# Two-layer cross-attention kernel: in the first layer, GpSimd issues the regrouping transfers, both halves of a projection share a step, and a batch's closing operations run some steps later

## The reference, cut to what matters

```
# layer 0, for each of 8 batches: x, kv are (256 channels, 512 positions), 16 heads of 16 channels
q = Wq @ x + bq;  k = Wk @ kv + bk;  v = Wv @ kv + bv
attn = softmax(q^T k / sqrt(16))                  # 512 x 512 for each head
mean = attn @ v;  ex2 = attn @ (v * v)
std  = sqrt(relu(ex2 - mean * mean))
x    = normalise(x) * std + mean                  # masked normalisation of x over positions
# layer 1, for each batch, x is (256 positions, 512 features), 16 heads of 32
x = x + self_attention(layernorm(x));  x = x + cross_attention(layernorm(x), ctx)
x = x + gelu(layernorm(x) @ w1 + b1) @ w2 + b2
```

## Time and profile before

| what | us |
|---|---|
| runs (3), median | 1876.81 |
| runs, lowest and highest | 1871.81, 1877.14 |
| profiled execution, its own time | 1867.23 |
| profiled execution, span of the trace | 1865.4 |
| last `maxima` of the first layer starts at | 727.8 |
| TensorE, VectorE, ScalarE, GpSimd busy | 1669.1, 1276.1, 1064.0, 342.7 |

### The profile page before, as it was taken

One profiled execution on the slowest core, in us unless ns is written; L12 is line 12 of the kernel. 1 busy time (PEld: TensorE's weight loads), 2 busy tenths in 40 slices (PEclk: granted clock), 3 DMA queues, 4 the chain that ended last, 5 costly groups with the idle time before them and its releaser, 6 DMA issues.

```text
span 1865.4 us, 30868 instructions
## 1 busy us (share of the span) xinstructions
PE 1669.1 (89%) x10589; PEld 1126.5 (60%) x10589; DVE 1276.1 (68%) x2758; ACT 1064.0 (57%) x2351; POOL 342.7 (18%) x435
## 2 busy tenths in 40 slices
PE   4888888887788889799999989999999899999999
PEld 2433333333333333478887877878888788888888
DVE  1666676676757766588899989999999864232322
ACT  1455556555555546678787787887878752121111
POOL 0001111112111113232223222223332130000000
PEclk7998898999989899999999999999999899999999
DMA  5343343444343433233223253333333240000000
GB/s 173 114 129 110 125 117 116 120 125 125 120 138 112 128 93 102 73 96 75 69 69 91 70 136 95 100 86 100 97 93 82 82 136 23 1 23 1 23 4 31
DMA packets 108955, 167.97 MB, mean 90 GB/s; under 512 B 23680, under 2 KB 39424, under 8 KB 108672
## 3 DMA queue, kind: packets, MB, share of 16 engines
q1 hardware_dynamic: 96784, 140.74, 26.4%
q0 software_dynamic: 9472, 20.99, 4.4%
q10 hardware_dynamic: 2544, 4.26, 0.8%
HBM read 72.06 MB, written 34.60 MB: 57 GB/s over the span
## 4 chain that ended last, share of the span: by engine, by line
PE 44%; DVE 20%; SPq 13%; DMA 10%; issue 7%; ACT 5%; POOL 1%; ACTq 0%; DVEq 0%; POOLq 0%
PE ps L1931 9%; PE ps L1905 7%; PE ps L526 6%; DMA ring<-rows 5%; DVE at_t L1383 4%; PE ps L1254 4%; DVE at_t L1388 4%; SPq L298 4%; SPq L366 3%; PE ps L1264 3%; PE ps L503 3%; SPq L332 2%; DMA rows<-shares_of 2%; PE ps L1203 2%; PE ps L1910 2%
## 5 line engine op out<-in xcount | busy, mean ns | idle before, releaser
L600 DVE TENSOR_REDUCE nmax<-ps 128x2 f32<-128x1024 f32 x256 | 311.2, 1221 | 204.5 <-PE ps L503 202.5
L772 ACT ACTIVATE prob<-ps 128x1024 f32<-128x1024 f32 x256 | 261.8, 1023 | 271.0 <-PE ps L512 267.5
L1591 ACT ACTIVATE at_prob<-at_t,at_nmax 128x256 f32<-128x256 f32 x512 | 256.6, 505 | 85.4 <-DVE at_nmax L1388 74.1
L526 PE MATMUL ps<-prob,v 128*64 128x512 f32 x1024 | 299.3, 665 | 0.9
L503 PE MATMUL ps<-ring 64*128 64x512 f32 x512 | 137.3, 533 | 117.7 <-issue 55.5
L1388 DVE CUSTOM_DVE_ANT_0 at_t<-at_t,at_off 128x256 f32<-128x256 f32 x512 | 232.3, 490 | 8.8
L503 PEld LDWEIGHTS ps<-ring 64*128 64x128 f32 x512 | 51.3, 196 | 275.2 <-issue 196.2
L2090 DVE CAST mlp_h_hi<-mlp_h 128x512 fp32r<-128x512 f32 x64 | 28.4, 444 | 212.0 <-ACT mlp_h L2002 180.0
L1749 POOL TENSOR_TENSOR at_low<-at_low,at_high 128x512 fp32r<-128x512 f32 x64 | 87.1, 1361 | 468.1 <-DVE at_high L1417 468.1
L2002 ACT ACTIVATE mlp_h<-ps,b 128x512 f32<-128x512 f32 x48 | 33.1, 690 | 218.4 <-PE ps L1905 218.4
L1203 PE MATMUL ps<-ident,at_prob 128*128 128x128 f32 x1024 | 156.9, 276 | 0.0
(11 more groups left out here) (215 smaller groups left out, 3747.1 us busy)
## 6 DMA issues: line engine op xcount, KB each, us to landing
ring<-rows SPq DMA_DIRECT2D x62, 512.0 KB, 4.7
rows<-shares_of SPq DMA_DIRECT2D x90, 256.0 KB
at_k_stack<-at_high SPq DMA_DIRECT2D x256, 64.0 KB, 2.5
at_q_stack<-at_high POOLq DMA_DIRECT2D x128, 64.0 KB, 2.5
at_q_stack<-at_high SPq DMA_DIRECT2D x128, 64.0 KB, 2.7
at_q_stack<-at_low SPq DMA_DIRECT2D x128, 64.0 KB, 2.1
at_k_stack<-at_low POOLq DMA_DIRECT2D x128, 64.0 KB, 2.4
c_in<-in_ctx SPq DMA_DIRECT2D x8, 512.0 KB, 4.6
```

What stands on the lines that cost most here:

```text
L526: mm = eng.matmul(ps[2 * QD * k:2 * QD * (k + 1), VB, :], v[:, c, HG * G + 2 * p + k, :], prob[:, M % PROBS, k, :], start=(c == 0), stop=( ...
L600: eng.tensor_reduce(nmax[:, n % 2, j, 2 * p:2 * p + 2], ps[:, at:at + 2, :], AX, ALU.max, negate=True).then_inc(s_max, 1)
L772: eng.activation(prob[:, M % PROBS, :, :], ps[:, ST:ST + 2, :], ACT.Exp, scale=float(HD0) ** -0.5).then_inc(s_exp, 1)
L1591: ins = eng.activation(prob[:, m % 2, i, :], t[:, p, i, :], ACT.Exp, scale=-1.0, bias=nmax[:, m % 4, i:i + 1], accum_out=z[:, T % 2, j, 2 ...
```

## The change

It touches only the first layer. Five things:

1. The two halves of a q projection both go into step 3, those of a k projection into step 6.
2. `regroup` becomes a function of the engine. GpSimd issues it for groups 0 to 29 (n < 60), SyncE for the last two groups, with semaphores of their own.
3. In the list of SyncE both `rows_out` stand at the end of the even group; `rows_in("q")` of the next group but one opens the odd group, ahead of `tops_in`; the other three `rows_in` follow directly. `shares_in` moves ahead of `tops_in`, and `far_out` ahead of `shares_out`.
4. The closing operations of a batch move to later steps on VectorE and ScalarE.
5. GpSimd's list interleaves regroups with its tensor operations.

```diff
-        if s in (2, 3, 5, 6) and w % 2 == 0 and w // 2 + 1 < PAIRS:
-            return [("q" if s < 4 else "k", w // 2 + 1, ((s + 1) % 3,))]
+        if s in (3, 6) and w % 2 == 0 and w // 2 + 1 < PAIRS:
+            return [("q" if s == 3 else "k", w // 2 + 1, (0, 1))]
...
+    def regroup(eng, n):
+        b, G, p = n // (2 * NG), n // 2 % NG, n % 2
+        eng.wait_ge(s_vout, n + 1)
...
+        done = (s_re if n < 2 * (GROUPS - 2) else s_last_re)[n % OUTS]
...
         for w in range(GROUPS + 3):
-            n, b, ahead = w - 2, w // NG - 1, w // 2 + 1
+            b, ahead = w // NG - 1, w // 2 + 1
+            if w % NG == 2 and b >= 0:
+                shares_in(b)
+            if w % 2 and ahead < PAIRS:
+                rows_in("q", 2 * ahead)
             if 0 <= w - 1 < GROUPS:
                 tops_in(w - 1)
-            if w % NG == 2 and b >= 0:
-                shares_in(b)
-            if 0 <= n < GROUPS:
-                regroup(2 * n)
+            if GROUPS <= w < GROUPS + 2:
+                regroup(eng, 2 * (w - 2))
             lead(w, False)
+            if GROUPS <= w < GROUPS + 2:
+                regroup(eng, 2 * (w - 2) + 1)
+            if w % 2 and ahead < PAIRS:
+                rows_in("k", 2 * ahead)
+                rows_in("q", 2 * ahead + 1)
+                rows_in("k", 2 * ahead + 1)
+            if w % NG == 2 and b + 2 < NB:
+                far_out(b + 2)
             if w % NG == 2 and b >= 0:
                 shares_out(b)
-            if w % NG == 2 and b + 2 < NB:
-                far_out(b + 2)
-            if w % 2 and ahead < PAIRS:
+            if w % 2 == 0 and ahead < PAIRS:
+                rows_out("q", ahead)
                 rows_out("k", ahead)
-                rows_in("q", 2 * ahead)
-                rows_in("k", 2 * ahead)
...
-            if 0 <= n < GROUPS:
-                regroup(2 * n + 1)
-            if w % 2 and ahead < PAIRS:
-                rows_in("q", 2 * ahead + 1)
-                rows_in("k", 2 * ahead + 1)
-            if w % 2 == 0 and ahead < PAIRS:
-                rows_out("q", ahead)
...
# VectorE
-                if w % NG == 2 and 0 <= b - 1 < NB and s == 3:
+                if w % NG == 2 and 0 <= b - 1 < NB and s == 5:
                     shares(b - 1)
-                if w % NG == 3 and 0 <= b - 1 < LAST - 1 and s == 5:
-                    positive_variance(b - 1)
-                if w % NG == 0 and 0 <= b - 2 < LAST - 1 and s == 2:
+                if w % NG == 0 and 0 <= b - 2 < LAST and s == 0:
+                    positive_variance(b - 2)
+                if w % NG == 0 and 0 <= b - 2 < LAST and s == (5 if w < GROUPS else 3):
                     normal_x(b - 2)
-                if w % NG == 1 and 0 <= b - 2 < LAST - 1 and s in (4, 5):
-                    last_mask(b - 2, s - 4)
...
+                if w % NG == 1 and 0 <= b - 2 < LAST and s in ((5, 6) if w < GROUPS else (2, 3)):
+                    last_mask(b - 2, (s + 1) % 3)
# ScalarE
-                if s == 3 and w % NG == 3 and 0 <= b - 1 < LAST - 1:
+                if s == 4 and w % NG == 3 and 0 <= b - 1 < LAST:
                     mean_squared(b - 1)
-                if s == 6 and w % NG == 3 and 0 <= b - 1 < LAST - 1:
-                    roots(b - 1)
...
+                if s == (2 if w < GROUPS else 1) and w % NG == 0 and 0 <= b - 2 < LAST:
+                    roots(b - 2)
# GpSimd
+        squares(0)
         for w in range(GROUPS):
+            n, b = w - 2, w // NG
+            if w % NG == 3 and 0 <= b - 1 < LAST:
                 finish_shares(b - 1, 0)
                 finish_shares(b - 1, 1)
+            if n >= 0:
+                regroup(eng, 2 * n)
+            if w % NG == 3 and 0 <= b - 1 < LAST:
                 finish_variance(b - 1)
             if w % NG == 0 and 0 < b < NB:
                 squares(2 * b)
+            if w % NG == 2 and b < NB:
+                squares(2 * b + 1)
+            if n >= 0:
+                regroup(eng, 2 * n + 1)
+            if w % NG == 0 and 0 <= b - 2:
                 finish_x(b - 2, 0)
                 finish_x(b - 2, 1)
```

More of the change, by code:

```diff
@@ L203, in layer0 @@
         s_re = [sem(f"re{k}") for k in range(OUTS)]
+        s_last_re = [sem(f"last_re{k}") for k in range(OUTS)]
         s_mask = sem("mask")
@@ L256, in regrouped, with all_regrouped @@
         def regrouped(n, k):
-            return (n - k + OUTS) // OUTS * 6 * DMA
+            times, by_pool = (n - k + OUTS) // OUTS, 2 * (GROUPS - 2) // OUTS
+            return [(s_re[k], min(times, by_pool) * 6 * DMA)] \
+                + ([(s_last_re[k], (times - by_pool) * 6 * DMA)] if times > by_pool else [])
+        def all_regrouped(eng, n):
+            for k in range(OUTS):
+                for done, value in regrouped(n, k):
+                    eng.wait_ge(done, value)
         def rows_of(i):
@@ L274, in layer0 @@
             "values out": [(s_vout, 2 * GROUPS)],
-            "regroups": [(s_re[k], regrouped(2 * GROUPS - 1, k)) for k in range(OUTS)],
+            "regroups": [x for k in range(OUTS) for x in regrouped(2 * GROUPS - 1, k)],
             "moments": [(s_fin, FINISH * LAST + 3)],
@@ L278, in layer0 @@
         }
+    def regroup(eng, n):
+        b, G, p = n // (2 * NG), n // 2 % NG, n % 2
+        eng.wait_ge(s_vout, n + 1)
+        if G == 0 and p == 0 and b >= 2:
+            eng.wait_ge(s_fin, FINISH * (b - 2) + 3)
+        done = (s_re if n < 2 * (GROUPS - 2) else s_last_re)[n % OUTS]
+        for k in range(2):
+            head = HG * G + 2 * p + k
+            at = HD0 * (head % (NH // 2))
+            base = 2 * QD * k
+            eng.dma_start(d["sums0"][b % 2, head:head + 1, :], v_out[base + 2 * HD0:base + 2 * HD0 + 1, n % OUTS, :])\
+               .then_inc(done, DMA)
+            for j, dst in enumerate((mean_in, second)):
+                eng.dma_start(dst[b % 2][at:at + HD0, G // 2, :], v_out[base + HD0 * j:base + HD0 * (j + 1), n % OUTS, :])\
+                   .then_inc(done, DMA)
     def sync(eng, lead):
@@ L283, in load @@
             eng.dma_start(X[:, b, :, :], d["x"][b].rearrange("(h p) t -> p h t", p=P)).then_inc(s_load[b % 2], DMA)
[L285 to L299, removed]
         def constants_out(k, src, done, first, last):
@@ L398, in shares_in @@
         def shares_in(b):
-            for k in range(OUTS):
-                eng.wait_ge(s_re[k], regrouped(2 * NG * (b + 1) - 1, k))
+            all_regrouped(eng, 2 * NG * (b + 1) - 1)
             eng.dma_start(z[:], d["sums0"][b % 2].rearrange("h (a e) -> (h a) e", a=P // NH)).then_inc(s_z, DMA)
@@ L741, in late @@
             if (run, m) == (0, 6):
-                for k in range(OUTS):
-                    eng.wait_ge(s_re[k], regrouped(2 * GROUPS - 1, k))
+                all_regrouped(eng, 2 * GROUPS - 1)
                 eng.wait_ge(s_rw, NB * SB * DMA)
@@ L805, in take_values @@
             if n >= OUTS:
-                eng.wait_ge(s_re[n % OUTS], n // OUTS * 6 * DMA)
+                for done, value in regrouped(n - OUTS, n % OUTS):
+                    eng.wait_ge(done, value)
             eng.activation(v_out[:, n % OUTS, :], ps[:, VB, :], ACT.Copy).then_inc(s_vout, 1)
@@ L900, in finish_shares @@
             if k == 0:
-                for k in range(OUTS):
-                    eng.wait_ge(s_re[k], regrouped(2 * NG * b + 2 * NG - 1, k))
+                all_regrouped(eng, 2 * NG * b + 2 * NG - 1)
                 eng.wait_ge(s_rw, (b + 1) * SB * DMA)
@@ L933, in gpsimd @@
                 squares(2 * b)
-            if w % NG == 0 and 0 <= b - 2 < LAST - 1:
+            if w % NG == 2 and b < NB:
[3 more added lines that the diff above has]
+            if w % NG == 0 and 0 <= b - 2:
                 finish_x(b - 2, 0)
                 finish_x(b - 2, 1)
[L937 to L941, removed]
         finish_x(LAST - 1, 0)
```

6 lines of the change are left out of this document (removed).

## The result

The changed kernel takes 1804.7 us in the median of four runs (1796.1 to 1808.1), where the kernel before took 1876.7. The ratio is 0.9615, with a 95% interval of 0.9576 to 0.9654: faster by 72 us. The forecast was 1763, 114 us faster, with a range of 1738 to 1812; the gain came, and 42 us of it were missing. The profiled execution has a span of 1806.2 us; against 1865.4 before, this is 59 us.

A forecast was written before the change was run, and what follows sets the result against it. The prediction took TensorE's waits for late ring rows, from the order in SyncE's queue, as the bound. Gains of 145 us less 32 lost, net 113, gave 1754 profiled and 1763 for the runs, range 1738 to 1812.

The forecast's parts named there:

- term of 124 us for the 14 stalls: TensorE's 14 waits for ring rows, with the slow steps after them, cost 8.9 us each and go: 124 us gained.
- half microsecond per pair kept for a remnant: Remaining stall on ring rows, a mean for groups with w%4=3 where slack is 0 to 1 us; 7 us lost.
- part 3: Both projection halves in one step: the wait of 1.81 us before the k half goes in six batches, 11 us gained.
- Rival D: GpSimd's issues locked out by VectorE, 1.7 us per transfer, so GpSimd sets the pace; 56 us slower, 1933; chance 0.03.
- B: A ring stall stays, as writes or the reads behind them take longer; net gain 47 us, 1830; chance 0.13.
- C: VectorE becomes the bound, losing 5 more us per batch, 35 us in all; 1798; chance 0.11.
- E: The wait shifts elsewhere, for instance to the tops behind `rows_in`, and nothing is won; 1877; chance 0.03.
- 7 x 1 = 7 us lost: In seven groups (7, 11, ...) tops behind `rows_in("q")` are issued about 1 us later; 7 us lost.
- part 4: Closing operations later: waits in group 31 go, about 5 us gained; against it, operations that lay beside a ring stall lose time.
- `roots` was put at 1 us in six groups: `roots` holds ScalarE, so at step 2 of w%4=0 an exponential comes about 1 us late; 6 us lost in all.
- `masks` was put at 1.4 in five groups: At step 6 of w%4=1 `masks` waits longer for `last_mask`; TensorE loses about 1.4 us five times, 7 us.
- The 5 us at the end of the layer: In group 31 the waits for `mean_squared` and `positive_variance`, with the slow clock behind, cost about 5 us and go.

The follow-up runs named there:

- closing_early: tops_first with the closing operations back at the steps of the kernel before; 1741.1 us, ratio 0.9300 to the kernel before.
- halves_split: tops_first with the projections' halves back in steps 2, 3, 5 and 6; 1760.1 us, ratio 0.9398 to the kernel before.
- tops_first: The changed kernel with the tops issued before the q read of the odd group; 1763.4 us, ratio 0.9421 to the kernel before.
- change_closing_early: The changed kernel, q read still ahead of the tops, with the closing operations back at their earlier steps; 1783.6 us, ratio 0.9529 to the kernel before.
- tops_pool: The changed kernel with the tops issued by GpSimd at the head of its list of each group; 1768.1 us, ratio 0.9448 to the kernel before.

## Why the prediction was right or wrong, point by point

**Right.** The bound was read rightly: order in SyncE's queue. The term of 124 us for the 14 stalls holds: none is left, the k rows are issued 0.8 us into group 17 (0.7 foretold), and the half microsecond per pair kept for a remnant wasn't needed. Its size fits too: closing_early, without most of what the change loses elsewhere, is 131 us faster than the kernel before, and the prediction's 124 and 11 of part 3 make 135. GpSimd's issues were taken at 0.496 us and measured 0.484, and neither TensorE nor ScalarE waits for regroups. Rival D took the lockout that it names to hold beside the maxima. But the Trainium skill, "SBUF — State Buffer", section "Who interferes with whom", says that `tensor_reduce` never contends with GpSimd on Trainium2, and the maxima are such instructions. The trace agrees: the longest of the 360 issues, beside maxima for the most part, took 0.667 us. So D rested on a misreading, and no run here was made to test the lockout itself. Rivals B, C, D and E fell: there is no ring stall, VectorE is busy for 57.7 of the 80.9 us of two pairs, and the time is well below that of before.

**Wrong: the tops.** The step that failed reads "`rows_in("q")` now stands ahead of the tops ... they would be issued about 1 us later relative to the group, so 7 x 1 = 7 us lost". It counted only when they are issued, and only where the queue is blocked, and it put even that too low: groups 7 to 27 with w%4=3 have the tops some 2 us later than before, not 1. The landing was not priced at all. The q read ahead of them makes it late, most plainly in the groups with w%4=1, where nothing had been put down: TensorE waits in seven of those eight as well. Together it is 47.0 us of idle time in 15 waits, and the low clock behind many of them, for 7 us in the sum. The right order is worth 41 us (36 by the ratios), about the whole gap between 1804.7 and the forecast's 1763. The prediction even looked at a queue's place for E ("the tops, behind `rows_in`, come as late as the rows do now"), and gave it 0.03.

**Wrong in cause, part 3.** The 11 us for the wait before k came, but from GpSimd's list, which the prediction had named beside the later step; halves_split shows that the halves had no part in it.

**Half right, part 4.** `roots` was put at 1 us in six groups; the step after it takes 3.15 us where 1.67 is plain, so 1.5. `masks` was put at 1.4 in five groups, and tops_first shows 1.55 in each; in the change most of them hide behind the waits for tops. The 5 us at the end of the layer didn't come. From the start of group 31 to its last `scores` it takes 18.4 us before and 18.7 with the change. From there to the end of the program the kernels with closing operations early take 1138.2 to 1139.2 us and those with them late 1140.6 to 1144.7 (the kernel before 1138.2, the change 1143.6), so the tail loses 5 us more. And the largest effect was missed: `shares` two steps later delays SyncE's list, 13 us in tops_first. The prediction had put the move of the closing operations at 10 us gained and 18 lost, and closing_early puts it at 22 us lost.

**That tops_first lands on 1763** is partly chance: it lacks the loss by the tops and the remnant of ring stalls, and has that by `shares` and the tail, which the prediction didn't have.

**What stays open.** Whether the gain of change_closing_early divides as in tops_first wasn't tried. Nor was a version with the tops in an otherwise idle hardware queue, which could say how much of the 30 us left in tops_pool is sharing of the transfer engines and how much is GpSimd's path; three times in tops_pool GpSimd itself began 3 us late, with nothing in the trace to account for it.

## What to carry to other kernels

When a transfer is moved ahead in a queue, price what is then behind it by its landing and not by its issue: a 4 KB transfer that TensorE needs in 5 us must not stand behind a 512 KB read that isn't needed for 18. Another queue is only half a remedy for that, as both are still under way at once; the large one has to be issued later. Moving small, frequent transfers out of a list that is waited for can be worth as much as a new order (66 us by itself; 40 for the rest of the change without it), and costs little if the other engine has the time. An operation whose result an in-order queue waits for is not free to be moved, however idle the engines around it: here two steps of one reciprocal cost 13 us.

## What the runs showed of the hardware that was not expected

A small transfer issued just behind a large one lands late. Tops issued 1.8 us after a 512 KB read were there 8.0 us after the issue of the first (group 17 of the change); in tops_first, with the k write 3.9 us ahead and the read behind, they were there within the 4.8 us until TensorE asked for them. `shares<-z`, 32 KB, took 1.5 us by itself and 6.8 in the median behind the q write of 768 KB.

The Trainium skill, "DMA: Bandwidth & Descriptors", section "Queues, rings and completion order", says that each transfer engine consumes the descriptors of one queue in ring order. By that rule the small transfer waits behind the read, and the 8.0 us agree with it. But the rule can't be all: issued from GpSimd, in a queue of their own, the tops of group 9 still took 6.0 us beside four such reads, against 8.2 behind one. How much is place in a queue and how much is sharing stays open.
